# Bias products padded to 128 rows, and the low part of the relu rows moved to GpSimd, in a graph and attention layer on one core

## The reference

```python
xn = _layernorm(x)
support = segment_sum(edge_weight[:, None] * xn[src], dst)       # gather, weight, add up
gnn = support @ W + bias
q = elu(xn @ Wq + bq) + 1;  k = elu(xn @ Wk + bk) + 1;  v = xn @ Wv + bv
mix = (linear attention with q, k, v over 8 heads) @ Wp + bp
x = x + gnn + mix
z = _layernorm(x)
g = mean over rows of (relu(z @ gfc1.T + gfc1_b) @ gfc2.T + gfc2_b)
W1m, b1m, W2m, b2m = weights merged from 8 experts by g
h = relu(z @ W1m.T + b1m)                                        # 256 columns
out = h @ W2m.T + b2m
res = z + out
x = x + layernorm(res) * lng + lnb
```

## Time and profile before

| | |
|---|---|
| median of 3 runs | 1598.65 us (1595.19 to 1599.21) |
| the profiled execution's own time | 1604.54 us |
| its span, first to last instruction | 1602.7 us |
| TensorE busy | 1385.1 us (86%) |
| VectorE busy | 1015.7 us (63%) |
| ScalarE busy | 648.3 us (40%) |
| GpSimd busy | 843.4 us (53%) |
| mean granted clock of TensorE | 0.946 of full speed |
| all transfers | 366.46 MB, 229 GB/s in the mean |

### The profile page before, as it was taken

The page is one execution under the profiler, slowest core; times in us unless marked ns, Lnnn a source line. Parts: engine busy times, 40 slices in busy tenths (PEclk is TensorE's granted clock), DMA queues, the critical chain, the costliest instruction groups (busy, mean ns, idle before and its releaser), DMA issues. The chain is left out here.

```text
span 1602.7 us, 24972 instructions
## 1 busy us (share of the span) xinstructions
PE 1385.1 (86%) x7963; PEld 605.9 (38%) x7963; DVE 1015.7 (63%) x2041; ACT 648.3 (40%) x1045; POOL 843.4 (53%) x882
## 2 busy tenths in 40 slices
PE   4988978898889888998898988998995998889893
PEld 2544423333333333333333433433342443633331
DVE  7978634344343434385666667877878675448997
ACT  4787722222222322033333323333333665256663
POOL 0001267777777777477777777777771000033432
PEclk9999989999999999699999999999997999899996
DMA  6989678888888888477777777777777879514432
GB/s 214 312 310 341 242 247 274 272 267 271 261 260 274 268 267 290 138 238 237 230 237 236 237 229 234 240 242 250 230 224 183 220 197 223 158 60 151 157 138 85
DMA packets 201553, 366.46 MB, mean 229 GB/s; under 512 B 77101, under 2 KB 82879, under 8 KB 201441
## 3 DMA queue, kind: packets, MB, share of 16 engines
q0 software_dynamic: 62720, 205.57, 41.9%
q1 hardware_dynamic: 138000, 158.43, 30.7%
q10 hardware_dynamic: 720, 1.06, 0.2%
HBM read 287.93 MB, written 65.38 MB: 220 GB/s over the span
## 5 line engine op out<-in xcount | busy, mean ns | idle before, releaser
L1165 POOL DMA_INDIRECT rows<-y_rows,idxT x516 | 492.4, 954 | 184.6 <-issue 165.7
L919 ACT ACTIVATE mb<-bank,ones,ncols 128x512 f32<-128x512 f32 x98 | 76.3, 779 | 445.8 <-PE bank L1964 445.8
L1519 DVE SCALAR_TENSOR_TENSOR acc<-bank,maskt,acc 128x512 f32 x196 | 138.0, 746 | 102.3 <-PE bank L2072 81.9
L2060 PE MATMUL bank<-rows,hots 128*32 128x512 f16 x1548 | 118.1, 412 | 55.5 <-DMA rows<-y_rows,idxT 47.2
L1964 PE MATMUL bank<-Wg,xtb 128*128 128x512 f16 x588 | 139.1, 388 | 16.1 <-DVE xtb L1453 8.9
L1964 PE MATMUL bank<-ztg,G 128*128 128x512 f16 (+1 forms) x624 | 130.7, 371 | 15.5 <-DMA ztg<-zhigh 14.1
L1964 PE MATMUL bank<-KVP,qT 128*128 128x512 f16 x588 | 143.9, 397 | 0.0
L1964 PE MATMUL bank<-Wk,xta 128*128 128x512 f16 x588 | 139.5, 388 | 0.0
L1964 PE MATMUL bank<-Wq,xta 128*128 128x512 f16 x588 | 139.2, 388 | 0.0
L1200 POOL TENSOR_TENSOR acc<-acc,lnbb 128x512 f32 (+1 forms) x49 | 66.0, 1349 | 116.4 <-ACT zq L1051 116.4
L2044 PE MATMUL bank<-xr,kh 128*128 128x512 f16 x392 | 123.7, 399 | 2.4 <-DVE kl L1546 2.4
(11 more groups left out here) (311 smaller groups left out, 2428.9 us busy)
## 6 DMA issues: line engine op xcount, KB each, us to landing
xta<-xt_rows SPq DMA_DIRECT2D x98, 256.0 KB
x_rows<-xhl SPq DMA_DIRECT2D x49, 256.0 KB, 3.8
xt_rows<-xtb SPq DMA_DIRECT2D x49, 256.0 KB, 3.9
y_rows<-yb SPq DMA_DIRECT2D x49, 256.0 KB, 3.6
xr<-x_rows SPq DMA_DIRECT2D x49, 256.0 KB
zt_rows<-ztg SPq DMA_DIRECT2D x49, 256.0 KB, 2.3
acc<-in_x SPq DMA_DIRECT2D x48, 256.0 KB, 4.2
xd<-zt_rows SPq DMA_DIRECT2D x12, 1024.0 KB, 5.4
```

Of the source, the lines that this page charges most:

```text
L919: nc.scalar.activation(mb[:, :], of[:, :], ACT.Relu, scale=ncols[:, col:col + 1], bias=ones[:, 0:1]).then_inc(f_min, 1)
L1165: pool.indirect_dma_start(out=row_slot(s, k).rearrange("p a d -> p (a d)"), out_offset=None, in_=y_rows, in_offset=bass.IndirectOffsetOnAx ...
L1519: nc.vector.scalar_tensor_tensor(out=flat(acc, tile + m), in0=edge_bank(n)[:, :], scalar=maskt[:, m, n:n + 1], in1=flat(acc, tile + m), op ...
L2060: ins = nc.tensor.matmul(edge_bank(n)[W * k:W * k + W, :], hots[:, r, p, :, hot_column(s, k)], row_slot(s, k)[:, q, :], start=s == FIRST[n ...
```

## The change

It has two parts.

1. The bias products are padded to full depth. `ones3`, `krows` and `qrows` become 128 rows high; `krows` and `qrows` are filled with zeros by two memsets at the start of GpSimd's program, and the three bias rows are then written over the first three. All 147 bias products (49 each of keys, queries and output) have 128 rows instead of 3. The counts that other engines wait for in `pool_set` rise by two.
2. In the last pass the low part of the relu rows is made by GpSimd (`hidden_rest`), except for the first group. So that one subtraction is enough, ScalarE's relu has the scale in it already: scale `cols[:, 7:8]` and bias `b1m[:, FC:]`, both multiplied by `scf[:, 2:3]` in two small instructions of VectorE ahead of the pass; the high part is then a plain copy. `hidden_rest` stands in the ticks j % 4 = 0 and 1, behind `add_base`, and not in 1 and 2 as on VectorE.

```diff
-        ones3 = put("ones3", [3, P], BF16)
+        ones3 = put("ones3", [P, P], BF16)
...
-        krows = put("krows", [3, D], BF16)
-        qrows = put("qrows", [3, D], BF16)
+        krows = put("krows", [P, D], BF16)
+        qrows = put("qrows", [P, D], BF16)
...
-                    at_least(act, low_made, H_LOW + FC * (q - 1) + o + 1)
-                    nc.scalar.activation(h32[:, o, 0:n], bank[2 + o][:, 0:n], ACT.Relu, scale=cols[:, 1:2],
-                                         bias=b1m[:, o:o + 1]).then_inc(high_made, 1)
+                    first = isinstance(q, int) and q == 1
+                    at_least(act, low_made, H_LOW + FC if first else H_LOW + FC * (q - 1) + o + 1)
+                    nc.scalar.activation(h32[:, o, 0:n], bank[2 + o][:, 0:n], ACT.Relu, scale=cols[:, 7:8],
+                                         bias=b1m[:, FC + o:FC + o + 1]).then_inc(high_made, 1)
                     act.wait_ge(high_made, H_HIGH + FC * q + o + 1)
-                    nc.scalar.activation(hT[:, par, 0, o, 0:n], h32[:, o, 0:n], ACT.Copy, scale=scf[:, 2:3]
-                                         ).then_inc(h_out, 1)
+                    nc.scalar.copy(hT[:, par, 0, o, 0:n], h32[:, o, 0:n]).then_inc(h_out, 1)
...
+            pool.memset(krows[:, :], 0.0).then_inc(pool_set, 1)
+            pool.memset(qrows[:, :], 0.0).then_inc(pool_set, 1)
...
+            def hidden_rest(g, j):
+
+                quad = quad_at(g, j)
+                if j % Q4 < FC and not (isinstance(quad, int) and quad + 1 >= NQ):
+                    par, n, o = (j // Q4 + 1) % 2, P if isinstance(quad, int) and quad + 1 == NQ - 1 else Q4 * P, j % Q4
+                    pool.wait_ge(h_out, FC * (quad + 1) + o + 1)
+                    waited(pool)
+                    nc.gpsimd.tensor_tensor(hT[:, par, 1, o, 0:n], h32[:, o, 0:n], hT[:, par, 0, o, 0:n], ALU.subtract
+                                            ).then_inc(low_made, 1)
...
+            def last_tick(g, j):
+                add_base(g, j)
+                hidden_rest(g, j)
+
+            row_ticks(pool, last_tick, T)
...
+            link(nc.vector.tensor_scalar(cols[:, 7:8], cols[:, 1:2], scf[:, 2:3], None, ALU.mult))
+            link(nc.vector.tensor_scalar(b1m[:, FC:], b1m[:, 0:FC], scf[:, 2:3], None, ALU.mult))
             dve.nop(nofuse=True).then_inc(scales_made, 1)
...
-                if j % Q4 in (1, 2) and not (isinstance(quad, int) and quad + 1 >= NQ):
-                    hidden_low(quad + 1, (j // Q4 + 1) % 2, P if isinstance(quad, int) and quad + 1 == NQ - 1 else Q4 * P,
-                               [j % Q4 - 1])
```

More of the change, by code:

```diff
@@ L334, in build @@
             ("gbr", [1, NE], F32), ("b1c", [P, FC], F32), ("tvb1", [P, FC, NE], F32),
-            ("b1m", [P, FC], F32), ("tvb2", [NE, D], F32), ("geye", [P, NE, P], F32))
+            ("b1m", [P, 2 * FC], F32), ("tvb2", [NE, D], F32), ("geye", [P, NE, P], F32))
         (W1raw, W2raw, lnrows, lbrows, g2raw, lngb, lnbb, lncoef, gjunk, gsum, gsq, gcol, gbias, g2T,
@@ L959, in _ @@
             act.wait_ge(y_low, T)
-            act.wait_ge(pool_set, 20)
+            act.wait_ge(pool_set, 22)
             for s in range(K_FIRST, SLOTS_END):
@@ L1105, in _ @@
                       allow_small_or_imprecise_dtypes=True).then_inc(pool_set, 1)
-            pool.wait_ge(pool_set, 15)
+            pool.wait_ge(pool_set, 17)
             for m in (ident, ident16):
@@ L1109, in _ @@
                                    pattern=[[-1, P]], channel_multiplier=1).then_inc(pool_set, 1)
-            pool.wait_ge(pool_set, 17)
+            pool.wait_ge(pool_set, 19)
             for b in range(2):
                 pool.memset(headmask[b * HD:(b + 1) * HD, b * HD:(b + 1) * HD], 1.0).then_inc(pool_set, 1)
-            pool.wait_ge(pool_set, 19)
+            pool.wait_ge(pool_set, 21)
             pool.nop(nofuse=True).then_inc(consts_made, 1)
@@ L1200, in add_base @@
                     pool.tensor_tensor(flat(acc, t), flat(acc, t), lnbb[:, :], ALU.add).then_inc(based, 1)
-            row_ticks(pool, add_base, T)
+            def last_tick(g, j):
+                add_base(g, j)
+                hidden_rest(g, j)
+            row_ticks(pool, last_tick, T)
         @block.vector
@@ L1670, in tile_at_group @@
                 return dve.value_load(tileof[0:1, n:n + 1], min_val=0, max_val=T - 2)
-            dve.wait_ge(pool_set, 20)
+            dve.wait_ge(pool_set, 22)
             for s in range(K_FIRST, SLOTS_END):
@@ L1836, in _ @@
                 link(nc.vector.tensor_tensor(tvb1[:, o, :], tvb1[:, o, :], gall[:, :], ALU.mult))
-            link(nc.vector.tensor_reduce(b1m[:, :], tvb1[:, :, :], AX_X, ALU.add))
-            link(nc.vector.tensor_tensor(b1m[:, :], b1m[:, :], b1c[:, :], ALU.add))
-            link(nc.vector.tensor_reduce(mx[:, 4:5], b1m[:, :], AX_X, ALU.max, apply_absolute_value=True))
+            link(nc.vector.tensor_reduce(b1m[:, 0:FC], tvb1[:, :, :], AX_X, ALU.add))
+            link(nc.vector.tensor_tensor(b1m[:, 0:FC], b1m[:, 0:FC], b1c[:, :], ALU.add))
+            link(nc.vector.tensor_reduce(mx[:, 4:5], b1m[:, 0:FC], AX_X, ALU.max, apply_absolute_value=True))
             merge_w2(0)
@@ L1889, in _ @@
             link(nc.vector.tensor_tensor(cols[:, 5:6], scf[:, 2:3], scf[:, 3:4], ALU.mult))
-            link(nc.vector.tensor_scalar(scale3[:, 0:P], ones3[:, :], cols[0:3, 5:6], None, ALU.mult))
+            link(nc.vector.tensor_scalar(scale3[:, 0:P], ones3[:, :], cols[:, 5:6], None, ALU.mult))
             def weights_low(o):
```

## The result

The changed kernel takes 1584.83 us in the median of five runs (1581.3 to 1587.5), the kernel before 1597.13 us in five runs of the same sitting (1594.09 to 1599.21). The ratio is 0.9921, with a 95% interval of 0.9899 to 0.9943: 12.3 us less. The prediction had said 1590.3 us, 8.3 us less than the runs shown with it. The two profiled executions lie further apart than the medians: 1604.54 us before, which is above all five runs, and 1587.50 us after; 17.0 us, or 17.1 between their spans.

A forecast was written before the change was run, and what follows sets the result against it. GpSimd's gather queue was taken to bound the key and query stages, VectorE the steady last pass. Terms of -1.2 - 0.9 - 6.2 + 0 = -8.3 us from 1598.65 gave 1590.3 us, 8-in-10 range 1583 to 1602.

The forecast's parts named there:

- What bounds the kernel now: Key and query stages: GpSimd's gather queue, so 19.6 us saved on TensorE gain nothing; steady last pass: VectorE, 13.66 us a group.
- Rival 3: Key and query stages: they gain after all because they wait for TensorE, -19.6 us more, 1571 us; chance 0.04.
- The bias product: All three stages: padding removes 0.20 us of TensorE's time per product, half before and half after; bounds 0 and 0.20.
- rival 4: Bias products: padding takes nothing away, the 0.20 us has another cause; -6.2 us in all, 1592.5 us; chance 0.07.
- At the start: Last pass before 1437 us: TensorE's products set the end, six padded bias products save 0.20 us each, -1.2 us.
- The wait of 1465.28: Last pass: VectorE's 1.78 us wait for TensorE shortens by half, -0.9 us; bounds 0 and -1.8.
- The low part: Steady last pass: moving hT's low part from VectorE to GpSimd saves 0.74 us a group over 8.4 groups, -6.2 us.
- The layout by hand: One steady group laid out instruction by instruction: 3.1 us of stall for six GpSimd instructions, 12.92 us a group.
- The end: After 1554 us: four subtractions leave VectorE, -1.9 us, stalls give about as much back: 0, bounds -1 and +2.
- The sum: Whole kernel: -1.2 - 0.9 - 6.2 + 0 = -8.3 us, 1590.3 us on the scale of the median.
- Rival 1: Steady last pass: new GpSimd instructions stall VectorE 0.65 us each, eating the gain; about 1597 us; chance 0.24.
- the memsets and VectorE's two tiny instructions: Start and before the last pass: memsets at most 0.52 us each, tiny instructions 0.19 each, all in idle time: 0.

The follow-up runs named there:

- e10: Kernel before with 128-row bias products of keys and queries only, last pass unchanged: 1596.2 us, ratio 0.9997 to the kernel before.
- e11: Kernel before with 128-row bias products in the last pass only: 1594.7 us, ratio 0.998 to the kernel before.
- e2: Changed kernel with three-row bias products everywhere, so only GpSimd's low part remains: 1588.03 us, ratio 0.9931 to the kernel before.
- e4: Changed kernel with three-row bias products of keys and queries, only the last pass padded: 1584.99 us, ratio 0.9924 to the kernel before.
- e9: Changed kernel with xd loaded two ticks earlier and bias products padded in the last pass only: 1575.84 us, ratio 0.9874 to the kernel before.
- e3: Changed kernel, all bias products padded, with xd loaded two ticks earlier, ahead of the out stores: 1578.89 us, ratio 0.9879 to the kernel before.
- e8: Changed kernel with xd loaded two ticks earlier and three-row bias products everywhere: 1580.39 us, ratio 0.9891 to the kernel before.
- e5: Kernel before with nothing changed but xd loaded two ticks earlier: 1598.68 us, ratio 1.0017 to the kernel before.
- e6: e3 with each of GpSimd's low-part subtractions done twice, the first into a spare tile: 1589.57 us in a single execution.
- e1: Kernel before with all bias products 128 rows deep, low part still on VectorE: 1598.66 us, ratio 1.0005 to the kernel before.
- e12: e1's kernel again, timed beside e11: 1593.83 us, ratio 0.9979 to the kernel before.

## Why the prediction was right, and where it was not

**What bounds the kernel now** held. The gathers stay 1.25 us apart, and the saved time of TensorE turned into waiting for them; the row of the key stage, 205 to 620 us, beside the earlier trace rows, where the wait was 31.7 us:

```profile
L2075 PE MATMUL bank<-rows,hots 128*32 128x512 f16 x600 | 45.7, 412 | 37.3 <-DMA rows<-y_rows,idxT 35.3 <-DVE hots L1526 2.0
```

With the 20.0 to 27.0 us of the same product in the query stage this is 12.6 us more, not the 20 that the prediction named, but all of it is waiting: none of the 19.6 us reached the time, as far as e10 can tell (0.9978 to 1.0016: at most 3.5 us). Rival 3 fell.

**The bias product** lost what was said, in all three stages. TensorE's timeline in the last pass of the changed kernel, then in the key stage of the kernel before and of the changed one:

```profile
1417.97 0.38 PE L1979 MATMUL bank<-krows,qrows 128*128 128x512 bf16 x1
1418.18 1.46 PE L1979 MATMUL bank<-W2m,hT 128*128 128x512 f16 x6
1419.48 0.38 PE L1979 MATMUL bank<-krows,qrows 128*128 128x512 bf16 x1
```

```profile
510.37 0.87 PE L2060 MATMUL bank<-rows_p,hots 128*32 128x512 f16 x12
511.18 0.39 PE L1964 MATMUL bank<-krows,ones 3*128 3x512 bf16 x1
511.50 2.76 PE L1964 MATMUL bank<-Wk,xta 128*128 128x512 f16 x12
```

```profile
513.14 0.87 PE L2075 MATMUL bank<-rows_p,hots 128*32 128x512 f16 x12
513.94 0.39 PE L1979 MATMUL bank<-krows,ones 128*128 128x512 bf16 x1
514.17 2.75 PE L1979 MATMUL bank<-Wk,xta 128*128 128x512 f16 x12
```

In the last pass the next product starts 0.21 us behind it, and the six products ahead of it take 1.30 us instead of 1.40: 0.20 us in all, with bf16 kept, so the type has no part in it and rival 4 fell. Behind a column-tiled product only the gap after it went: the way to it is 0.81 us before and 0.80 after, the way from it 0.32 and 0.23. That is the half that the prediction took from the Trainium skill, "TensorEngine Tiling (Array Packing)", Key Properties; the trace agrees.

**At the start** -1.2 us were predicted to tile 5. From tile 0 to tile 5, over five of these products, it is -1.04 us, in after and in e11 alike, and 0 in e2. **The wait of 1465.28** The earlier trace rows was taken for half, -0.9; it went entirely. e11, where nothing else was changed, has -1.86 from tile 5 to 13. So on the kernel before the padding is worth 3 us and not 2.1, and the term that was mis-sized is this half. In e2 the wait went too, by the other way: that stretch is 3.9 us shorter there. The two parts share this wait, and their gains don't simply add up.

**The low part.** The layout by hand gave 3.1 us of stall for six GpSimd instructions and a group of 12.92 us. The trace has 3.16 us of stall, and from tile 13 to 41 a group of 12.96 us (90.69 / 7). That is nearer than it deserves. For one thing, the layout was set against two scales: against its own 13.79 us for the kernel before it says -0.87 a group, against the trace's 13.66 it says -0.74, and the prediction took the latter without a reason. For another, one step is missing: the load of xd. The prediction looked at every wait that TensorE had and asked what came next; it named `res`. It did not follow SyncE's queue, where the load stands behind a store that waits for `ob`, and there the next wait was. TensorE's 6.8 us in five groups reach VectorE only as 1.2 us. But once, at 1510.87, TensorE had waited 1.99 us, and then its clock fell. Timeline of TensorE, and below it its stretches of 4 us around that point (the granted clock is the third figure from the end):

```profile
1510.87 4.45 PE L1979 MATMUL bank<-xd,W1m 128*128 128x512 f16 x12 [1.99 <-DMA xd<-zt_rows]
```

```profile
1508.00:1512.00 4.00, 2.01 (x10) 0.75 (x8) 3.60 (x8) 2.85 (x6) 4.00 (x3) 0.97 0.76 282
1512.00:1516.00 4.00, 4.00 (x12) 1.46 (x11) 3.76 (x6) 2.12 (x5) 4.00 (x3) 0.61 0.17 66
```

The twelve products take 4.45 us instead of 2.76 and the group 14.66 us; between 1512 and 1516 the clock is 0.61, part of that time at its lower level of 1.2 GHz. The wait alone doesn't explain the fall. A longer one in the same trace was followed by products at full speed:

```profile
1485.20 2.76 PE L1979 MATMUL bank<-xd,W1m 128*128 128x512 f16 x12 [2.21 <-DMA xd<-zt_rows]
```

And the traces of e2 and e4, which wait for xd too, have no such fall between 1416 and 1548 us. What set it off is open. It is the main part of the 1.8 us by which the stretch from tile 13 to 41 is longer after (90.69) than in e4 (88.92), where the last pass is the same.

With xd early the group is 12.25 us, and the last pass from tile 0 on another 3.7 us shorter (e9 against e4) or 5.1 us (e3 against after, whose trace has the fall of the clock).

So the gain of the low part, rid of xd, is 13.57 - 12.25 = 1.32 us a group: the whole 1.33 that left VectorE. Of this pair e3 is padded and the kernel before is not; e8 and e5, neither of them padded and both with xd early, give 13.57 - 12.30 = 1.27. Two more instructions on GpSimd cost VectorE next to nothing (2.7 us of stall a group before, 2.8 in e3). GpSimd paid, its additions going from 1.35 to 1.72 us, and it had the time. Its subtraction, sized at 1.15 us, took 1.16 undisturbed and 1.43 in the mean (1.53 in e3). Of the bounds of the prediction (-1.96 to +1.2 a group) the measured value is in the lower half. From 6 to 8 GpSimd instructions a group (e6) the price is 0.58 each: by then GpSimd is busy for 65.6 of 71 us and has little time left to be the one that waits.

**The end** was taken for 0, between -1 and +2. It is -2.65 us (-2.8 in e2), outside the bounds, and this is the term that was furthest off. Groups by shape, VectorE, the last 36 us before and the last 33 us after:

```profile
L1938 DVE SCALAR_TENSOR_TENSOR ob<-cen,rsr,acc 128x512 f32<-128x512 f32 x13 | 14.3, 1101 | 1.2
L1928 DVE SCALAR_TENSOR_TENSOR cen<-res,negm,lngb 128x512 f32<-128x512 f32 x13 | 11.4, 877 | 0.1
```

```profile
L1956 DVE SCALAR_TENSOR_TENSOR ob<-cen,rsr,acc 128x512 f32<-128x512 f32 x13 | 12.9, 993 | 1.2
L1946 DVE SCALAR_TENSOR_TENSOR cen<-res,negm,lngb 128x512 f32<-128x512 f32 x13 | 12.4, 957 | 0.1
```

The prediction let the stalls give back the 1.9 us of the four instructions that leave. They gave back nothing: cen and ob together took 25.7 us before and 25.3 after. With the 1.9 us this makes 2.3 of the 2.65; the last 0.3 is not accounted for. The rows of that stretch of before have one addition for each tile, as the steady part has, and nothing in them spoke for a dearer one.

**The sum** for the last pass was -8.3 us; it is -1.04 - 4.44 - 4.32 - 2.65 = -12.45 us by the landmarks, and 12.3 by the medians. The sign, the place and the mechanism held. The 4.1 us that were missing are the end (2.65) and the stretch from tile 5 to 13 with the wait of 1465.28 (4.44 instead of 0.9 and 1.9 groups at 0.74, which is 2.3), less 0.5 in the stretch after it (4.32 instead of the 6.5 groups left of the 8.4, 4.8) and 0.2 at the start. Without the waits for xd the gain would have been 4 to 5 us more. Rival 1 (0.65 us for each instruction) would have left the group at 13.6, and the memsets and VectorE's two tiny instructions cost nothing that can be seen.

## What to carry to other kernels

When a wait is taken away, the next one is often not on the two engines that were looked at but in a queue beside them: follow every transfer that the waiting engine needs back to the instruction that stands ahead of it in its queue, and ask when that one is released. The stalls between two engines that exclude each other need not grow with each instruction. Here, as long as GpSimd had time to spare, it was the one that waited more, and two instructions moved onto it for nearly nothing; with it nearly full, two more cost 0.58 us each. And a part of a trace that differs between two executions in a stage that the change can't reach should be looked for in other kernels' traces before it is explained.

## What the hardware did that was not expected

- GpSimd's instructions and VectorE's with two SBUF inputs alternated. With three and more of GpSimd's back to back (e6) no ob between 1440 and 1545 us took more than 1.69 us and no cen more than 1.48, so none was passed over. The Trainium skill ("SBUF — State Buffer", Who interferes with whom) says that whoever issues first holds the pair of ports for the whole instruction; the rows agree in the main (a stalled ob of 0.75 us ends 0.55 us after GpSimd's instruction), and they add that in these traces the side that waited came next.
- The mean granted clock was a little lower in most kernels with 128-deep products in the key and query stages (0.950 in e1 and e10, 0.951 in e12, 0.952 after) than in those without (0.954 in e11, 0.955 in e4, 0.956 in e8, 0.957 in e2, 0.958 in e9), and 0.953 to 0.955 in the kernel before. But e3, which has them too, stands at 0.954, as high as e11. No time that could be measured went with it. Whether the depth is the cause, and how, is open.
- The wait of the gathers at the turn differs by 13 us between executions (2.3 to 15.3 us) of kernels whose work there is the same. In the main it goes with TensorE's clock from 616 to 668 us: 0.76 in the kernel before, 0.80 to 0.87 in the four other traces with waits of 6.9 to 10.2 us, 0.86 to 0.92 in the nine with 2.3 to 4.6. What sets that clock was not tried.
